# Three hand-written orders for the run-up, the steady and the last bodies of a pipelined transformer block

## The chip, the cores and the metric

The kernel runs on one core of one Trainium2 chip. The metric is the device time of one execution in microseconds. Each kernel is one launch; times are compared between runs on the same chip.

## What is computed

The input is x of 16 batches, 512 tokens each, with 128 features (f32). Three residual steps follow each other:

```python
x = x + linear_attention(layernorm(x)) @ W_out.T   # 16 heads of 8; Chebyshev orders 1..5 of clipped q and k;
                                                   # running sums over the tokens, numerator / denominator
x = x + softmax_attention(layernorm(layernorm(x))) # causal, 16 heads of 8; its own norm with ln1_g, ln1_b
n = layernorm(layernorm(x))                        # last norm with ln2_g, ln2_b
top, idx = top_k(n @ gate_W + gate_b, 2); w = softmax(top)
x = x + sum over the two experts of w * (gelu(n @ W1[e] + b1[e]) @ W2[e] + b2[e])   # 8 experts, 512 hidden
```

## The kernel before

**Two halves.** The first half (until about 1070 us of the trace) runs both attentions and the gate for every batch and sends each token's normed row, with its weight and its number, to a list per expert in HBM (`xg`), by indirect DMAs. The second half runs the experts over 39 blocks of 512 rows from these lists, sends their outputs back to pairs per token, and adds the pairs at the end.

**The software pipeline.** `pipelined(body)` (L327 to L330) calls the body of each engine for t = -5 to 15. One body works on six batches at once, one in each stage; a stage whose batch does not exist is None and is left out:
- f = t+5: first norm (POOL `ln_rsqrt("a")`, ACT `apply0`), projections, clip, and the Chebyshev orders of k and q (`third_order`, `even_orders` L1153/L1154 on POOL, `fifth_order` L536).
- h = t+4: `head_sums` of k and q (PE L1320, ten matmuls of 512 columns on 32 partitions, five for each), `sum_k` (DVE L553, L564), products and running sums (`times_v` L550, `sum_kv` L553, POOL `times_q` L1162, `add_products` L1173), `output1` (L1344, L1355), `add_x1`, the second norm ("m", `ln_rsqrt` in its long form on POOL), ACT `apply1` and `apply2` (both L480; `apply2` writes `ha`).
- g = t+3: `turn_ln`, q, k, v of the softmax attention, and q and k split into three bf16 parts (DVE `third_part` L593, POOL `less_first_part` L1183). SP writes the parts to `spread` in HBM and from there the 'stack' of rows that the scores are products of (L388 to L393); its second half waits until all 48 scores of the body are done.
- m = t+2: the row maxima of the scores, needed ahead of the exponentials. 44 steps: PE `maximum` (L1393, L1395) and DVE's reduction (`nm`, L599). `max_rest` (DVE L602 to L604) and `max_parts` (ACT) turn each half of the maxima into two bf16 rows `nms`, and `put_maxima` (ACT L977) writes them by DMA into the stack. Half 0 belongs to heads 0 to 7, half 1 to heads 8 to 15.
- b = t+1: 48 `scores` (PE L1433, L1435), 48 `exps` (ACT L986), 12 `values` (PE L1452), `evacuate` (ACT L990), four times `turn_back` and `normalise` (DVE L610, L612), `take_y` (ACT L994, the last piece of a batch; its starts mark the bodies here). `scores` 0 waits for half 0 of the stack and of the maxima, `scores` 24 for half 1.
- t: `output2` (PE L1477), `x2` (DVE L621), third norm ("b", POOL L447 to L473), `apply3` (ACT L480, into `rows`), `turn_x2`, gate, `gate_top` and `gate_weights` (DVE L628 to L656), `ranks`, `slots` (DVE L658 to L671, slot numbers `sloti`), ACT `copy_rows` (L1007), and eight indirect DMAs (POOL `dispatch`, L1197), four for each of the two chosen experts, each with 128 rows.

**What sets the order.** Nothing schedules at run time but semaphores: each engine issues its instructions in program order. PE, ACT and DVE walk 129 slots per body. The tables MAX_PE, SCORES_PE, VALUES_PE, MAX_DVE, EXPS_ACT and LEAVE_ACT (L310 to L319) say in which slot each repeated step stands, `at(n, stage)` says it for the single steps, and POOL's and SP's bodies are written out. The order is the same for every t. For example `put_maxima(m, p, 0)` stands at slot 83 of ACT, where 48 of 48 exponentials are already issued.

**The gate's weights.** `gate_weights` computes 1/(1+e) and e/(1+e) in the columns of `gt`, copies both into `rows` (L655), compares the indices with the expert numbers in two instructions (L651), and advances the tokens' numbers in `rows` by 1024 (L656).

## Time and profile before

| what | value |
|---|---|
| device time, median of 3 runs | 1379.57 us (1373.16 to 1382.08) |
| the profiled execution's own time | 1373.93 us |
| span of the profiled execution | 1372.1 us |
| busy, share of the span | PE 83%, DVE 79%, ACT 68%, POOL 61% |
| mean granted TensorE clock | 0.91 |
| run-up bodies (t = -5 to -1) | 0 to 207.4 us |
| steady bodies (t = 0 to 11) | 207.4 to 891.8 us |
| last bodies, three of four (t = 12 to 14), then t = 15 | 891.8 to 1035.3, then to 1070.8 us |
| experts, then the final sums | 1070.8 to 1310, then to 1372.1 us |

PE is TensorE, DVE VectorE, ACT ScalarE, POOL GpSimd, SP SyncE. A body is the stretch from one `take_y` (L994) to the next. PEclk is the granted clock of TensorE as a share of full speed; the two levels are 1.2 and 2.4 GHz, so a stretch at 0.97 spent part of its time at the lower one. A wait in the view of waits names the engine and line that stood idle and what ended it.

### The profile page before, as it was taken

The numbers are of one execution on the slowest core, as the hardware profiler recorded it, in microseconds if no ns is written. First come the engines' busy times: TensorE is split into PE (matmuls) and PEld (weight loads), VectorE is DVE, ScalarE is ACT, GpSimd is POOL, SyncE is SP. The second block draws the span as 40 slices with busy tenths as digits, with TensorE's granted clock in tenths as the row PEclk, the third lists the DMA queues.
The fourth block names the chain that finished last, engine by engine and source line by source line (L and its number), as shares of the span: only waits on it lengthen the run. The fifth ranks groups of instructions, "written<-read, shape, count | busy, mean of one in ns | idle before, by whom it ended". The sixth has DMA issues, their size and how long they took to land.

```text
span 1372.1 us, 27932 instructions
## 1 busy us (share of the span) xinstructions
PE 1141.6 (83%) x8883; PEld 702.2 (51%) x8883; DVE 1086.1 (79%) x2555; ACT 934.1 (68%) x1859; POOL 841.7 (61%) x1105
## 2 busy tenths in 40 slices
PE   3546898998989989889898998988893799999960
PEld 1223354454644546445464454544452588888840
DVE  4557888898988989899898897965715688888845
ACT  2334487696876968769687695675574699999940
POOL 2775566776877767777777686532224166666660
PEclk9677799999999999999999999988985899999985
DMA  9231231423324223142241422413232222222239
GB/s 207 50 88 51 49 88 30 109 72 60 97 51 105 72 58 101 31 115 78 58 103 41 96 77 44 104 62 73 84 127 104 78 79 85 84 86 82 67 139 367
DMA packets 84436, 121.91 MB, mean 89 GB/s; under 512 B 15270, under 2 KB 66522, under 8 KB 80002
## 3 DMA queue, kind: packets, MB, share of 16 engines
q1 hardware_dynamic: 70978, 98.07, 27.5%
q0 software_dynamic: 9088, 17.33, 3.6%
q10 hardware_dynamic: 4224, 4.72, 1.1%
q8 instruction: 71, 1.16, 0.4%
q14 instruction: 75, 0.61, 0.2%
HBM read 63.96 MB, written 57.46 MB: 88 GB/s over the span
## 4 chain that ended last, share of the span: by engine, by line
PE 65%; DMA 12%; DVE 10%; ACT 7%; issue 5%; POOL 1%; ACTq 1%; SPq 0%; POOLq 0%; DVEq 0%
PE back L1452 8%; PE front L1586 8%; PE back L1598 8%; DMA stack<-nms 7%; PE scores L1433 6%; PE front L1320 6%; PE maxima L1393 5%; ACT pr L986 4%; DVE nm L599 3%; PE scores L1435 3%; PE front L1295 3%; PE maxima L1395 3%; PE back L1270 2%; DMA stack<-pairs 2%; PE front L1477 1%
## 5 line engine op out<-in xcount | busy, mean ns | idle before, releaser
L986 ACT ACTIVATE pr<-scores 128x384 f32<-128x384 f32 (+1 forms) x768 | 369.6, 523 | 144.1 <-PE scores L1435 137.3
L599 DVE TENSOR_REDUCE nm<-maxima 128x1 f32<-128x384 f32 (+3 forms) x704 | 420.5, 631 | 44.4 <-PE maxima L1395 38.4
L1433 PE MATMUL scores<-stack 65*128 65x384 bf16 (+2 forms) x768 | 205.6, 285 | 57.3 <-DMA stack<-nms 32.6
L1393 PE MATMUL maxima<-stack 65*128 65x128 bf16 (+2 forms) x768 | 197.7, 282 | 16.2 <-DVE nm L599 14.5
L1197 POOL DMA_INDIRECT xg<-rows,sloti x128 | 137.0, 1070 | 108.0 <-DVE sloti L669 44.0
L1395 PE MATMUL maxima<-stack 128*128 128x128 bf16 x1024 | 182.6, 224 | 6.7 <-DMA stack<-spread 5.1
L1435 PE MATMUL scores<-stack 128*128 128x128 bf16 x1024 | 181.3, 225 | 0.0
L1452 PE MATMUL back<-pr,vaug 128*9 128x512 f32 (+3 forms) x2048 | 178.4, 444 | 1.5 <-ACT oT L990 1.0
L1433 PEld LDWEIGHTS scores<-stack 65*128 65x128 bf16 x768 | 75.6, 98 | 179.3 <-ACT pr L986 106.8
L1259 POOL DMA_INDIRECT pairs<-xs x104 | 111.0, 1068 | 78.7 <-DVE xs L832 51.9
L1393 PEld LDWEIGHTS maxima<-stack 65*128 65x128 bf16 x768 | 74.7, 98 | 121.9 <-DVE nm L599 87.4
L1586 PE MATMUL front<-h_first,w_now 128*128 128x512 f32 x312 | 126.2, 405 | 2.7 <-DVE h_second L812 2.5
L1127 ACT ACTIVATE xs<-front,b1p 128x512 f32<-128x512 f32 x156 | 107.5, 689 | 18.8 <-PE front L1586 16.6
L1162 POOL TENSOR_TENSOR kv<-F,kv 128x512 f32<-128x512 f32 x80 | 100.6, 1283 | 27.6 <-DVE kv L553 27.6
L1395 PEld LDWEIGHTS maxima<-stack 128*128 128x128 bf16 x1024 | 94.5, 100 | 29.9 <-issue 22.0
L1598 PE MATMUL back<-hid_first,w_now 128*128 128x512 f32 x312 | 96.3, 390 | 0.0
L1435 PEld LDWEIGHTS scores<-stack 128*128 128x128 bf16 x1024 | 92.4, 100 | 5.8 <-issue 4.6
L553 DVE TENSOR_TENSOR_SCAN kv<-one,front 128x512 f32<-128x512 f32 x80 | 93.7, 1204 | 0.0
L1320 PE MATMUL front<-F,cst 128*32 128x512 f32 x320 | 81.9, 804 | 3.9 <-DVE F L536 3.5
L1173 POOL TENSOR_TENSOR kv<-kv 128x512 f32<-128x512 f32 x64 | 80.4, 1267 | 2.4
L1153 POOL TENSOR_SCALAR F<-F 128x512 f32<-128x512 f32 x32 | 48.2, 1507 | 53.6 <-DVE F L532 53.3
L825 DVE TENSOR_TENSOR hid_second<-xs,hid_first 128x512 fp32r<-128x512 f32 x99 | 68.0, 687 | 15.7 <-ACT hid_first L1108 14.9
(219 smaller groups left out, 2459.5 us busy)
## 6 DMA issues: line engine op xcount, KB each, us to landing
stack<-spread SPq DMA_DIRECT2D x32, 400.0 KB
spread<-qs SPq DMA_DIRECT2D x96, 128.0 KB
spread<-ks SPq DMA_DIRECT2D x96, 128.0 KB
stack<-spread SPq DMA_DIRECT2D x32, 384.0 KB
xs<-xg SPq DMA_DIRECT2D x39, 272.0 KB, 2.9
stack<-pairs SPq DMA_DIRECT2D x8, 1024.0 KB, 13.5
stack<-in_consts SPq DMA_DIRECT2D x4, 1280.0 KB
xg<-xs SPq DMA_DIRECT2D x17, 272.0 KB
```

Of the source, the lines that this page charges most:

```text
L599: v.tensor_reduce(nm[:, h:h + heads, t], ring(n)[:, 0:heads * (t + 1) * P].rearrange("p (h n) -> p h n", h=heads), AX.X, ALU.max, negate=T ...
L986: a.activation(pr[:, n % PR, 0:width], ringE[n % 2][:, 0:width], ACT.Exp).then_inc(W.exp_ready, 1)
L1197: g_.indirect_dma_start(xg[:, :], bass.IndirectOffsetOnAxis(sloti[:, i, q:q + 1], 0), rows[:, i, q, :], None).then_inc(W.dispatched, 16)
L1259: g_.indirect_dma_start(pairs[:, :], bass.IndirectOffsetOnAxis(xt[i % XT][:, at:at + 1].bitcast(U32), 0), yo[i % 3][:, q * D:(q + 1) * D], ...
L1320: last = k.matmul(dst[32 * j:32 * j + 32, :], cst[:, C_SUM + 32 * var:C_SUM + 32 * var + 32], z[p], start=(p < 4), stop=(p > 0), skip_grou ...
L1393: k.matmul(ring(n)[:, at:at + t * P], qst[p][0:OPEN_ROWS, h, own], kst[p][0:OPEN_ROWS, h, 0:t * P], start=(j == 0), stop=True, skip_group_ ...
L1395: last = k.matmul(ring(n)[:, at + t * P:at + (t + 1) * P], qst[p][:, h, own], kst[p][:, h, own], start=(j == 0 and t == 0), stop=True, ski ...
L1433: k.matmul(dst[:, at + P:at + T - t * P], kst[p][0:OPEN_ROWS, h, own], qst[p][0:OPEN_ROWS, h, (t + 1) * P:T], start=(t == tiles[0]), stop= ...
L1435: last = k.matmul(dst[:, at:at + P], kst[p][:, h, own], qst[p][:, h, own], start=False, stop=True, skip_group_check=True)
L1452: last = k.matmul(V[32 * i:32 * i + DH + 1, t * P:T], vaug[:, b % VR, t, 4 * (s_ // 3) + i, :], pr[:, (4 * s_ + i) % PR, at:at + T - t * P ...
L1586: last = k.matmul((X, Y)[n % 2][:, :], w_now[:, i % 2, wi, c * P:(c + 1) * P], h2p[hi][:, i % 2, :], start=(j == 0), stop=(j == len(TERMS3 ...
L1598: last = k.matmul((Z, V)[i % 2][:, :], w_now[:, i % 2, 2 + wi, c * P:(c + 1) * P], (hidh, hidl)[hi][i % 2 * HC + c], start=(c == 0 and j = ...
```

## The change

- `pipelined` hands each body a number w: 0 for t below 0, 1 for t = 0 to 11, 2 for t = 12 to 15. Every table and every single place becomes a triple, one order for each w.
- GpSimd's body is also placed by slots (26 of them), three orders.
- The places of the split expert weights move (SPLIT_DVE, SPLIT_ACT; only in the body t = 15).
- `gate_weights` writes the reciprocal and the product straight into `rows`, compares with one instruction of 128x64, and leaves the numbers to a new `next_ids` on GpSimd; `dispatch` waits for the weights and the numbers apart.
- `turn_ln` (PE) also waits for `x2` of the batch t.

```diff
-        gt = sb("gt", [P, 4, QT])
+        gt = sb("gt", [P, 2, QT])
...
-        SLOTS = 129
+        SLOTS, POOL_SLOTS = 129, 26
...
-        MAX_DVE = (1, 3, 5, 9, 11, 14, 15, 18, 23, 25, 27, 28, 29, 31, 32, 34, 35, 36, 38, 39, 40, 41, 44, 45, 49, 50, 53, 54, 56, 57,
...
+        MAX_DVE = ((8, 9, 10, 12, 15, 16, 18, 19, 20, 22, 23, 24, 26, 27, 28, 29, 30, 32, 33, 34, 35, 36, 37, 38, 41, 43, 45,
...
...
-        SPLIT_DVE, SPLIT_ACT = (8, 21, 52, 55), (0, 2, 32, 58, 60, 66, 72, 75)
+        SPLIT_DVE, SPLIT_ACT = (20, 36, 45, 52), (17, 24, 58, 64, 76, 80, 84, 87)
...
         def pipelined(body):
 
             for t in range(-5, B):
-                body(*(t + i if 0 <= t + i < B else None for i in range(6)), (t + 1) % 2)
+                body(*(t + i if 0 <= t + i < B else None for i in range(6)), (t + 1) % 2, (t >= 0) + (t >= 12))
...
             def gate_weights(b):
                 dve.wait_ge(W.g_exp, b + 1)
                 v.tensor_scalar(gd[:, :], gt[:, 1, :], 1.0, None, ALU.add).then_inc(W.g_step, 1)
-                dve.wait_ge(W.g_step, b * 4 + 2)
-                v.reciprocal(gt[:, 2, :], gd[:, :]).then_inc(W.g_step, 1)
-                dve.wait_ge(W.g_step, b * 4 + 3)
-                v.tensor_tensor(gt[:, 3, :], gt[:, 1, :], gt[:, 2, :], ALU.mult).then_inc(W.g_step, 1)
+                dve.wait_ge(W.g_step, b * 3 + 2)
+                v.reciprocal(rows[:, 0, :, R_W], gd[:, :]).then_inc(W.g_step, 1)
                 dve.wait_ge(W.topi_ready, b * QT + QT)
-                dve.wait_ge(W.g_step, b * 4 + 4)
-                for i in range(2):
-                    v.tensor_tensor(oh[:, i, :, :], cst[:, C_IO:C_IO + E].unsqueeze(1).to_broadcast((P, QT, E)),
-                                    topi[:, :, i:i + 1].to_broadcast((P, QT, E)), ALU.is_equal).then_inc(W.oh_ready, 1)
-                dve.wait_ge(W.oh_ready, b * 2 + 2)
+                v.tensor_tensor(oh[:, :, :, :], cst[:, C_IO:C_IO + E].unsqueeze(1).unsqueeze(1).to_broadcast((P, 2, QT, E)),
+                                topi[:, :, 0:2].rearrange("p t i -> p i t").unsqueeze(3).to_broadcast((P, 2, QT, E)),
+                                ALU.is_equal).then_inc(W.oh_ready, 1)
+                dve.wait_ge(W.g_step, b * 3 + 3)
+                v.tensor_tensor(rows[:, 1, :, R_W], gt[:, 1, :], rows[:, 0, :, R_W], ALU.mult).then_inc(W.meta_ready, 1)
+                dve.wait_ge(W.oh_ready, b + 1)
                 v.tensor_tensor(chosen[:, :, :], oh[:, 0, :, :], oh[:, 1, :, :], ALU.add).then_inc(W.mask_ready, 1)
-                v.tensor_copy(rows[:, :, :, R_W], gt[:, 2:4, :]).then_inc(W.meta_ready, 1)
-                v.tensor_scalar(rowsi[:, :, :, R_ID], rowsi[:, :, :, R_ID], float(2 * T), None, ALU.add).then_inc(W.meta_ready, 1)
 
...
-                    at = lambda place, stage: n == place and stage is not None
+                    at = lambda places, stage: n == places[w] and stage is not None
...
+                    if at((68, 2, 3), t):
+                        x2(t)
...
+                    if at((1, 4, 81), h):
+                        sum_k(h)
...
+                    if at((40, 45, 47), m):
+                        max_rest(m, 0)
...
+                    if at((51, 80, 19), f):
                         fifth_order(f, kx, W.k_sq, W.k_t35)
...
+                    if at((5, 10, 16), t):
                         apply3(t)
...
+                    if at((28, 49, 36), t):
                         copy_rows(t)
...
+                    if at((77, 75, 70), m):
                         put_maxima(m, p, 0)
...
+            def next_ids(t):
+                if t == 0:
+                    pool.wait_ge(W.meta_ready, 2)
+                g_.tensor_scalar(rowsi[:, :, :, R_ID], rowsi[:, :, :, R_ID], float(2 * T), None, ALU.add).then_inc(W.ids_ready, 1)
+
             sent = [0]
 
             def dispatch(t, i, tiles):
                 wait_apart(pool, W.slot_ready, t + 1)
                 wait_apart(pool, W.h_copied, t + 1)
-                wait_apart(pool, W.meta_ready, t * 2 + 4)
+                wait_apart(pool, W.meta_ready, t + 3)
+                wait_apart(pool, W.ids_ready, t + 1)
...
-            def body(t, b, m, g, h, f, p):
-                if t is not None:
-                    add_residual(t)
-                    ln_rsqrt("b", t)
-                if h is not None:
-                    times_q(h, (0,))
-                if f is not None:
-                    ln_rsqrt("a", f)
-                if h is not None:
-                    times_q(h, (1,))
-                    times_q(h, (2,))
-                    times_q(h, (3,))
-                    times_q(h, (4,))
-                    add_products(h, (0, 1))
-                if g is not None:
-                    less_first_part(g, 0)
-                    less_first_part(g, 1)
-                if h is not None:
-                    add_products(h, (2, 3))
-                if t is not None:
-                    dispatch(t, 0, (0,))
-                    dispatch(t, 0, (1,))
-                    dispatch(t, 0, (2,))
-                if f is not None:
-                    even_orders(f, kx, W.k_t35, W.k_t24)
-                if t is not None:
-                    dispatch(t, 0, (3,))
-                    dispatch(t, 1, (0,))
-                    dispatch(t, 1, (1,))
-                if f is not None:
-                    even_orders(f, qx, W.q_t35, W.q_t24)
-                if h is not None:
-                    ln_rsqrt("m", h)
-                if t is not None:
-                    dispatch(t, 1, (2,))
-                    dispatch(t, 1, (3,))
-                if h is not None:
-                    keep_residual(h)
-                if t is not None:
-                    wait_apart(pool, W.dispatched, t * (16 * 2 * QT) + 16 * 2 * QT)
-                    pool.sem_inc(W.rows_free, 1)
+            def body(t, b, m, g, h, f, p, w):
+                for n in range(POOL_SLOTS):
+                    at = lambda places, stage: n == places[w] and stage is not None
+                    if at((21, 0, 4), t):
+                        ln_rsqrt("b", t)
+                    if at((1, 1, 2), t):
+                        next_ids(t)
+                    if at((2, 2, 3), t):
+                        add_residual(t)
+                    if at((3, 3, 23), f):
+                        ln_rsqrt("a", f)
+                    if at((4, 4, 10), h):
+                        times_q(h, (0,))
+                    if at((6, 5, 22), h):
+                        times_q(h, (1,))
+                    if at((9, 6, 14), h):
+                        times_q(h, (2,))
+                    if at((11, 7, 7), h):
+                        times_q(h, (3,))
+                    if at((16, 8, 8), h):
+                        times_q(h, (4,))
+                    if at((15, 9, 24), h):
+                        add_products(h, (0, 1))
+                    if at((12, 10, 6), g):
+                        less_first_part(g, 0)
+                    if at((18, 11, 15), h):
+                        add_products(h, (2, 3))
+                    if at((14, 12, 9), g):
+                        less_first_part(g, 1)
+                    if at((5, 13, 5), t):
+                        dispatch(t, 0, (0,))
+                    if at((8, 14, 11), t):
+                        dispatch(t, 0, (1,))
+                    if at((7, 15, 12), t):
+                        dispatch(t, 0, (2,))
+                    if at((25, 16, 13), t):
+                        dispatch(t, 0, (3,))
+                    if at((0, 17, 16), t):
+                        dispatch(t, 1, (0,))
+                    if at((10, 18, 17), t):
+                        dispatch(t, 1, (1,))
+                    if at((20, 19, 1), f):
+                        even_orders(f, kx, W.k_t35, W.k_t24)
+                    if at((17, 20, 19), t):
+                        dispatch(t, 1, (2,))
+                    if at((13, 21, 20), t):
+                        dispatch(t, 1, (3,))
+                    if at((22, 22, 18), f):
+                        even_orders(f, qx, W.q_t35, W.q_t24)
+                    if at((23, 23, 21), h):
+                        ln_rsqrt("m", h)
+                    if at((24, 24, 0), h):
+                        keep_residual(h)
+                    if at((19, 25, 25), t):
+                        wait_apart(pool, W.dispatched, t * (16 * 2 * QT) + 16 * 2 * QT)
+                        pool.sem_inc(W.rows_free, 1)
...
-            def turn_ln(g, h):
+            def turn_ln(g, h, t):
                 pe.wait_ge(norm["m"]["out"], g * 8 + 8)
+                if t is not None:
+                    pe.wait_ge(W.x2_ready, t + 1)
                 if h is not None:
...
+                    if at((114, 3, 3), t):
                         output2(t, h)
+                    if at((0, 4, 66), h):
                         head_sums(h, kx, X, W.k_t24, W.k_t35, W.ks_mm, W.x1_ready, h)
+                    if at((2, 5, 17), h):
                         head_sums(h, qx, Y, W.q_t24, W.q_t35, W.qs_mm, *((W.x2_ready, t + 1) if t is not None else (W.outT_ready, h)))
+                    if at((33, 40, 5), g):
+                        turn_ln(g, h, t)
...
```

The orders themselves, as the two programs issue them. First ACT at the end of a steady body. The pr rows are exponentials (`exps`), the DMA rows are `put_maxima`, hs and ha are `apply1` and `apply2`, hn is `take_y`. Before:

```order
L986 ACTIVATE pr<-scores 128x512 x2
L990 ACTIVATE oT<-back 128x512
L986 ACTIVATE pr<-scores 128x384 x8
L977 DMA stack<-nms 1x32x128 x2
L990 ACTIVATE oT<-back 128x512
L480 ACTIVATE hs<-xs,morem,rstdm 128x128 x4
L972 ACTIVATE nms<-back 32x128
L994 ACTIVATE hn<-back 128x512
L977 DMA stack<-nms 1x32x128 x2
L480 ACTIVATE ha<-xs,morem 128x128 x4
```

After:

```order
L1003 ACTIVATE pr<-scores 128x512 x2
L1007 ACTIVATE oT<-back 128x512
L1003 ACTIVATE pr<-scores 128x512
L1003 ACTIVATE pr<-scores 128x384
L994 DMA stack<-nms 1x32x128 x2
L1003 ACTIVATE pr<-scores 128x384 x7
L1007 ACTIVATE oT<-back 128x512
L500 ACTIVATE hs<-xs,morem,rstdm 128x128 x4
L989 ACTIVATE nms<-back 32x128
L1011 ACTIVATE hn<-back 128x512
L994 DMA stack<-nms 1x32x128 x2
```

The first `put_maxima` moved from behind the last exponentials to a place ahead of the last seven; the rest of the body's end is as it was.

Second, PE in the run-up, in the body t = -2, the first that has maxima. The maxima rows are `maximum`, which read the stack, the front rows from L1320 (after: L1358) are `head_sums`. Before:

```order
L1344 MATMUL front<-rdT,cst 128x128 x4
L1355 MATMUL front<-wo_sb,outT 128x128 x4
L1395 MATMUL maxima<-stack 128x128 x4
L1393 MATMUL maxima<-stack 128x128
L1395 MATMUL maxima<-stack 128x128
L1393 MATMUL maxima<-stack 128x128
L1395 MATMUL maxima<-stack 128x128
L1320 MATMUL front<-F,cst 32x512 x5
L1393 MATMUL maxima<-stack 128x128
```

After:

```order
L1382 MATMUL front<-rdT,cst 128x128 x4
L1393 MATMUL front<-wo_sb,outT 128x128 x4
L1358 MATMUL front<-F,cst 32x512 x10
L1435 MATMUL maxima<-stack 128x128 x4
L1433 MATMUL maxima<-stack 128x128
L1435 MATMUL maxima<-stack 128x128
L1433 MATMUL maxima<-stack 128x128
```

All ten matmuls of `head_sums` now stand ahead of the first maximum; before, two maxima steps stood ahead of the first five.

Third, DVE at the gate of a steady body. The nm rows are reductions of the maxima; L643 to L656 (after: L663 to L673) is `gate_weights`. Before:

```order
L599 TENSOR_REDUCE nm<-maxima 128x1
L599 TENSOR_REDUCE nm<-maxima 128x4
L599 TENSOR_REDUCE nm<-maxima 128x2
L643 TENSOR_SCALAR gd<-gt 128x4
L645 RECIPROCAL gt<-gd 128x4
L647 TENSOR_TENSOR gt<-gt 128x4
L651 TENSOR_TENSOR oh<-cst,topi 128x32 x2
L654 TENSOR_TENSOR chosen<-oh 128x32
L655 COPY rows<-gt 128x8
L656 TENSOR_SCALAR rows<-rows 128x8
L599 TENSOR_REDUCE nm<-maxima 128x2
```

After:

```order
L619 TENSOR_REDUCE nm<-maxima 128x2 x2
L663 TENSOR_SCALAR gd<-gt 128x4
L665 RECIPROCAL rows<-gd 128x4
L667 TENSOR_TENSOR oh<-cst,topi 128x64
L671 TENSOR_TENSOR rows<-gt,rows 128x4
L673 TENSOR_TENSOR chosen<-oh 128x32
L619 TENSOR_REDUCE nm<-maxima 128x1 x2
```

Three instructions are gone from DVE (one of two comparisons, the copy and the addition), and the weights are written where the dispatch reads them.

## Rows read from the trace of the kernel before

**Rows 1.** Windows by stage; columns: window, length, busy us and count per engine, PEclk, DMA share.
```profile
0.00:207.40 207.40, 131.87 (x777) 67.05 (x777) 141.02 (x286) 90.65 (x184) 122.55 (x178) 0.79 0.39 89
207.40:891.80 684.40, 625.53 (x5670) 349.51 (x5667) 613.05 (x1535) 510.16 (x1104) 499.48 (x696) 0.97 0.31 75
891.80:1035.30 143.50, 127.88 (x1167) 71.81 (x1164) 73.96 (x225) 92.58 (x198) 39.63 (x58) 0.88 0.30 91
1035.30:1070.80 35.50, 5.65 (x28) 4.60 (x29) 19.41 (x67) 14.24 (x26) 13.97 (x19) 0.51 0.24 84
```

**Rows 2.** Windows of single steady bodies, columns as in rows 1.
```profile
379.50:434.90 55.40, 50.67 (x476) 28.74 (x474) 51.19 (x130) 43.00 (x94) 42.87 (x59) 1.00 0.33 80
...
549.80:608.10 58.30, 53.72 (x476) 29.80 (x474) 51.26 (x130) 43.11 (x94) 42.88 (x59) 0.94 0.31 75
...
720.70:776.50 55.80, 50.82 (x477) 28.80 (x474) 51.33 (x130) 43.16 (x95) 42.26 (x60) 1.00 0.29 74
```

**Rows 3.** Waits of PE, bodies 3 to 12: us in total, times, longest.
```profile
PE scores L1433 <- DMA stack<-nms: 22.8, 10, 2.7
```

**Rows 4.** Chain of waits, 435 to 492 us: start, us, what.
```profile
429.99 7.29 DMA stack<-nms
```

**Rows 5.** Windows around one body's end, columns as in rows 1.
```profile
430.00:433.50 3.50, 3.13 (x34) 1.43 (x30) 3.31 (x9) 1.32 (x3) 2.29 (x10) 1.00 0.91 177
...
439.00:442.00 3.00, 3.00 (x10) 0.35 (x2) 1.09 (x2) 0.51 (x2) 2.34 (x3) 0.52 0.17 52
```

**Rows 6.** Timeline of ACT and POOL, one body's second half: start, us, what.
```profile
403.05 0.48 ACT L986 ACTIVATE pr<-scores 128x384 f32<-128x384 f32 x1
403.42 0.63 ACT L1007 ACTIVATE rows<-rows 128x512 f32<-128x512 f32 x1
...
413.23 1.10 POOL L1197 DMA_INDIRECT xg<-rows,sloti  x1 [0.16 <-issue]
...
419.38 1.51 POOL L1153 TENSOR_SCALAR F<-F 128x512 f32<-128x512 f32 x1 [1.51 <-DVE F L532]
...
437.38 1.65 ACT L480 ACTIVATE ha<-xs,morem 128x128 f32<-128x128 f32 x4 [1.87 <-POOL morem L473]
...
439.43 0.96 POOL L1197 DMA_INDIRECT xg<-rows,sloti  x1 [0.30 <-issue]
```

**Rows 7.** Groups of DVE by line, bodies 3 to 12: busy, mean ns, idle before.
```profile
L599 DVE TENSOR_REDUCE nm<-maxima 128x1 f32<-128x512 f32 (+3 forms) x440 | 262.6, 630 | 10.8 <-PE maxima L1395 6.9 <-DVE xs L584 0.5
...
L553 DVE TENSOR_TENSOR_SCAN ksum<-one,front 128x512 f32<-128x512 f32 x10 | 12.2, 1221 | 16.3 <-PE front L1320 16.3
...
L621 DVE TENSOR_TENSOR x2t<-front,xs 128x512 f32<-128x512 f32 x10 | 6.9, 692 | 18.4 <-PE front L1477 18.4
...
L665 DVE TENSOR_TENSOR oh<-oh,slot 128x64 f32<-128x64 f32 x10 | 3.1, 306 | 0.0
L651 DVE TENSOR_TENSOR oh<-cst,topi 128x32 f32<-128x32 f32 x20 | 2.9, 188 | 1.0
...
L656 DVE TENSOR_SCALAR rows<-rows 128x8 int32<-128x8 int32 x10 | 1.7, 169 | 0.0
L655 DVE COPY rows<-gt 128x8 f32<-128x8 f32 x10 | 1.7, 169 | 0.0
```

**Rows 8.** Groups of POOL by line, same stretch and columns.
```profile
L447 POOL TENSOR_SCALAR lnva<-mva 128x4 f32<-128x4 f32 x9 | 5.1, 569 | 0.8
...
L447 POOL TENSOR_SCALAR lnvb<-mvb 128x4 f32<-128x4 f32 x10 | 2.3, 232 | 30.9 <-DVE mvb L437 30.9
```

**Rows 9.** Waits of PE in the run-up, 0 to 207.4 us.
```profile
PE maxima L1395 <- DMA stack<-spread: 5.1, 1, 5.1
...
PE front L1320 <- DVE F L536: 3.5, 1, 3.5
```

**Rows 10.** Chain of waits, 0 to 208 us.
```profile
60.44 6.56 PE front L1320 x20
```

**Rows 11.** Waits of PE, last three bodies, 891.8 to 1035.3 us.
```profile
PE scores L1433 <- DMA stack<-nms: 5.5, 3, 2.1
```

More of the change, by code:

```diff
@@ L738, in body @@
[L738 to L748 removed]
+                    if at((39, 43, 53), g):
+                        third_part(g, 2, kf, ks)
@@ new lines, in body @@
+                    if at((42, 44, 80), f):
+                        clip(f, kx, W.hk_ev, W.k_clip)
+                    if at((40, 45, 47), m):
+                        max_rest(m, 0)
+                    if at((48, 47, 76), f):
+                        clip(f, qx, W.hq_ev, W.q_clip)
+                    if at((47, 51, 60), g):
+                        third_part(g, 1, qf, qs)
+                    if at((50, 53, 71), f):
+                        third_order(f, kx, W.k_sq, W.k_t35)
+                    if at((44, 54, 49), b):
+                        normalise(b, 0)
@@ L1014, in first_weights, with body @@
                 a.activation(w2p[0][:, e * HC:(e + 1) * HC, :], w2_sb[:, e * HC:(e + 1) * HC, :], ACT.Copy).then_inc(W.wh_ready, 1)
-            def body(t, b, m, g, h, f, p):
+            def body(t, b, m, g, h, f, p, w):
                 for n in range(SLOTS):
-                    at = lambda place, stage: n == place and stage is not None
+                    at = lambda places, stage: n == places[w] and stage is not None
                     if b is None and t is not None and n in SPLIT_ACT:
@@ new lines, in body @@
+            def body(t, b, m, g, h, f, p, w):
+                for n in range(POOL_SLOTS):
+                    at = lambda places, stage: n == places[w] and stage is not None
+                    if at((21, 0, 4), t):
[51 more added lines that the diff above has]
+                        pool.sem_inc(W.rows_free, 1)
@@ L1501, in ranks, with body @@
                 last.then_inc(W.rank_mm, 1)
-            def body(t, b, m, g, h, f, p):
+            def body(t, b, m, g, h, f, p, w):
                 for n in range(SLOTS):
-                    at = lambda place, stage: n == place and stage is not None
-                    if m is not None and n in MAX_PE:
-                        maximum(m, MAX_PE.index(n), 1 - p)
-                    if b is not None and n in SCORES_PE:
-                        scores(b, SCORES_PE.index(n), p)
-                    if b is not None and n in VALUES_PE:
-                        values(b, VALUES_PE.index(n))
-                    if at(3, t):
+                    at = lambda places, stage: n == places[w] and stage is not None
+                    if m is not None and n in MAX_PE[w]:
+                        maximum(m, MAX_PE[w].index(n), 1 - p)
+                    if b is not None and n in SCORES_PE[w]:
+                        scores(b, SCORES_PE[w].index(n), p)
+                    if b is not None and n in VALUES_PE[w]:
+                        values(b, VALUES_PE[w].index(n))
+                    if at((114, 3, 3), t):
```

242 lines of the change are left out of this document (108 added, 134 removed), and 20 rows, old and new, of tables (EXPS_ACT, MAX_DVE, MAX_PE, SCORES_PE).

## The prediction

> **What bounds the kernel now.** I read the windows by stage first, then the waits of PE (TensorE), then the chain of waits, and last the groups by line. In the steady bodies PE is busy 625.5 of 684.4 us, DVE (VectorE) 613.1 [rows 1]. PE is the engine with the least room, and two things stand beside its work. One is a wait in every body: `scores` 0 waits for the DMA of the row maxima, 22.8 us in ten bodies, 2.3 each [rows 3]. The other is its clock: the bodies at clock 1.00 take 55.4 and 55.8 us (first and last of three), one at 0.94 takes 58.3 with DVE's work the same 51.2 to 51.3 [rows 2]. The lower clock comes right behind the wait: at the end of one body PE is at 1.00 (430 to 433.5), and in 439 to 442, behind its wait, at 0.52, so nearly all at 1.2 GHz, with PE busy all the time [rows 5]. So the steady loop loses 2.3 us to the wait, and 57.0 - 55.6 = 1.4 us per body, 17 us in twelve, to the clock (684.4/12 = 57.0; 55.6 is the middle of the two rows).
>
> Why is the DMA late? It takes 7.3 us from issue to landing [rows 4], and it lies in a stretch where the DMA engines are busy 0.91 of the time [rows 5]: SP's loads of the next stack start when the last scores are done, at the same moment. It is issued late because `put_maxima` of half 0 stands behind all 48 exponentials in ACT's order, although the maxima of that half are done far earlier.
>
> **Steady bodies, PE.** The change moves this issue ahead of the last seven exponentials. Seven of them take at least 7 x 0.48 us (one of this shape) [rows 6], and they are paced by PE, so the DMA starts 3.4 us earlier or more, I take 5, out of the crowd; I expect the wait of 2.3 us gone. With it should go the clock's fall. PE's floor is then 55.6 - 2.3 = 53.3 us per body: -3.7, or -44.7 in twelve. That is the upper end of the gain.
>
> **Steady bodies, DVE.** PE won't reach it, since DVE is next: it is busy 51.2 of 57.0, idle 5.8. The edits to the gate take from it the copy (0.169), the addition (0.169), and of two comparisons (2 x 0.188) 0.376 - 0.306 = 0.07, with L665 as the row for an instruction of 128x64: 0.4 us together, at most 0.17 + 0.17 + 0.19 = 0.53, at least 0.34 [rows 7]. Busy is then 50.8. Of the 5.8 us idle, x2's wait for `output2` is 1.8, the first running sum's wait for `head_sums` 1.6, the waits of the maxima's reductions 1.1 [rows 7]; 1.3 is spread. In the new order scores 0, two maxima, `output2` and both `head_sums` open the body, so the two waits at its start shrink (I take 0.4 left of 3.4), but only two maxima stand ahead of the sums; the third and fourth maxima of PE are in slots 12 and 20, and DVE, which gets to them early, will wait for them: about 1.4, and 0.7 more at `max_rest`. With the rest as it is (1.1 + 0.5) this makes 4.1. The body is then 50.8 + 4.1 = 54.9, or -2.1, which is -25.6 in twelve. The ends: nothing if all idle time comes back elsewhere, -44.7 if DVE hides behind PE.
>
> **GpSimd.** `next_ids` is new on POOL: 8 numbers per partition. The nearest rows are POOL's small instructions, 0.23 and 0.57 us [rows 8]; I take 0.4, with 17 us of idle per body (499.5 busy of 684.4 for twelve is 41.6 of 57.0 each) as the cover [rows 1]. If the cover went, it would be 5 us in twelve.
> The row for `lnva` (0.57) against the same operation on `lnvb` (0.23) shows that such an instruction is stretched by what runs beside it [rows 8]. The Trainium skill, "SBUF — State Buffer", section "Who interferes with whom", says why it can: a DVE instruction with two SBUF inputs and a GpSimd instruction that reads SBUF hold one shared port pair by an exclusive lock, and the later of them blocks. By that rule part of the 0.4 us saved on DVE returns as blocking, 0.2 per body, and the sum would be 2.4 us less gain; by the rows alone it is as above.
>
> **Run-up (207.4 us at a clock of 0.79 [rows 1]).** Two waits of PE are aimed at. In the body t = -2 the first maxima wait 5.1 us for the first load of the stack [rows 9]. Now all ten `head_sums` matmuls stand ahead; 20 of them took 6.6 us [rows 10], so 3.3 for each of k and q with the later ones done at once: they fill 4 to 5 of the 5.1. I take -4.5. In an earlier body `head_sums` waits 3.5 us for `fifth_order` [rows 9], which for k now stands behind `third_order` at slot 51 and not at 80; I take -2.5. Sums ahead of maxima on DVE and the rest: -1. Together -8, ends 0 and -15, since the new orders differ in every slot.
>
> **Last bodies (143.5 us, clock 0.88 [rows 1]).** The same DMA costs 5.5 us in three bodies [rows 11], and the clock 127.9 x (1 - 0.88) = 15.3. The wait goes; the clock comes back by half, 7.6, since ACT's exponentials pace these bodies too and small gaps stay. `turn_ln` moves to slot 5 in t = 12, where it waits for x2 and `apply2`: +2. That is -11, ends -3 and -20. The body t = 15 (35.5 us, PE busy 5.7 [rows 1]) is a chain of norm, gate, ranks and eight dispatches; the gate loses 0.4 us of that chain and `next_ids` leaves it: 0 to -1, taken as 0. The experts and final sums are untouched.
>
> **The sum.** -25.6 - 8 - 11 = -44.6 on the profiled execution's own 1373.9 (span 1372.1 and 1.8 around it) is 1329.3. The median of the runs stands 5.7 above that execution, so I put the forecast at 1333, between 1329.3 and the 1335.0 that the median gives.
> By the Trainium skill, "TensorE: Matmul & The Clock Gate", section "HAM oscillation — how this bites in real kernels", the loss is half of the throttled time. In 684.4 us at 0.97, half speed held for 2 x 0.03 x 684.4 = 41 us, so the loss is 20.5 where the bodies' lengths give 17; the sum would be 3 us lower if all of it came back.
>
> **Rivals.**
> (a) PE reaches its floor: DVE's idle time hides and steady bodies take 53.3. For it speaks that PE leads DVE in every view now; against, that DVE would have to be idle for 53.3 - 50.8 = 2.5 us only, less than half of today's 5.8. -44.7 - 8 - 11: 1310 to 1315; with the outer ends of the other two terms, 1298.
> (b) The order gives back what the DMA gave: DVE's new wait for PE's slots 12 and 20, or a maxima DMA that lands no earlier, keeps steady bodies at 57.0, and run-up and last bodies bring half. -9.5: 1370. For it speaks that DVE's idle time is only 5.8 and the new order has new waits. If the wait for stack<-nms still stands in PE's waits, this is the cause.
> (c) Slower: the tail on GpSimd. `copy_rows`, which the dispatches wait for, ran 23.9 us into its body (403.4 - 379.5) [rows 6, 2] with 22 exponentials ahead of it; now 30 stand ahead, which at the same pace is +33.6. Behind it on POOL, in order, stand eight dispatches, both `even_orders` and the norm "m", and then ACT's `apply2` and the exponential 0 of the next body. From the first dispatch to `apply2` was 24.15 us (413.23 to 437.38), less a wait of 1.5; two dispatches stood behind it and were done 3.0 us later (439.43 + 0.96); with `apply2` 1.65 and an exponential 0.5 that is 24.15 - 1.5 + 3.0 + 2.15 = 27.8 [rows 6]. 33.6 + 27.8 = 61.4, or 6.5 us into the next body of 54.9. `output2` and both `head_sums` fill PE until some +6 (1 us and 20 matmuls, 6.6 at half clock, stand in front [rows 10]). So it just fits. If the dispatches, now in one row, cost 0.3 more each, or `copy_rows` slips by 2, PE stands still at scores 2 of every body and its clock falls with each: +3 for the wait and +1.4 for the clock, less the old 2.3: about +2.1 per body or +25, less 8 and 3 elsewhere: 1394. It decides from a tail of 30 us.
> (d) The orders for the run-up and the last bodies bring nothing, those for the steady bodies do: 1373.9 - 25.6 = 1348, by the median 1354.
>
> **How the numbers follow.** Chances: the forecast with its own range of 1320 to 1350, 0.56; (a) 0.09; (b) 0.14; (c) 0.10; (d) 0.11. A measurement of this kernel can tell about 1%, 13.8 us: faster is below 1365.8, slower above 1393.4. Forecast, (a), (d) and a little of (b) are faster, 0.77; the rest of (b) and a part of (c) the same, 0.14; the rest slower, 0.09. The range of 8 in 10 reaches from 1300, most of (a), to 1370, the near half of (b).
>
> **What would show it.** In the profile after: no wait scores <- DMA stack<-nms above 0.3 us per body; granted clock 0.99 or 1.00 in the steady windows; bodies of 54 to 56 us; DVE busy 50.8 in each; reductions (nm) with more idle time before them than 1.1 and `x2` and `ksum` with less; no wait of PE for the stack above 1 us in the run-up; last three bodies some 132 us. A wait of scores <- ACT pr near the start of each body, behind apply2, would show (c). I am wrong if steady bodies stay above 56.5, or if the clock stays below 0.97 with the DMA wait gone.

## The result, and the profile after

The changed kernel took 1344.03 us (median of 4 runs, 1335.16 to 1344.48) beside 1379.02 for the kernel before; the ratio is 0.974, 95% interval 0.9695 to 0.9785. The forecast was 1333 with a range of 1300 to 1370, faster with 0.77. The profiled execution has a span of 1342.3 us, 29.8 less than before.

The windows by stage of the changed kernel (columns as in rows 1):

```profile
0.00:206.50 206.50, 136.72 (x769) 70.07 (x770) 144.42 (x286) 90.52 (x183) 125.30 (x176) 0.77 0.38 89
206.50:871.80 665.30, 619.84 (x5670) 352.98 (x5671) 606.28 (x1500) 514.40 (x1104) 511.15 (x710) 0.97 0.31 77
871.80:1006.30 134.50, 122.77 (x1172) 72.00 (x1170) 73.72 (x215) 92.13 (x197) 40.07 (x63) 0.92 0.33 101
1006.30:1040.00 33.70, 4.73 (x28) 3.76 (x28) 18.88 (x64) 14.24 (x26) 13.54 (x18) 0.57 0.19 65
```

Against rows 1 the run-up gives 0.9 us, the steady bodies 19.1, the last three 9.0 and the body t = 15 1.8; the experts and the final sums take 1.0 more. The granted clock of the steady stage is still 0.97. Three of its bodies, against rows 2:

```profile
315.40:369.60 54.20, 50.34 (x473) 29.07 (x473) 50.51 (x126) 43.28 (x94) 43.68 (x61) 1.00 0.33 80
...
593.50:649.20 55.70, 51.87 (x473) 29.19 (x473) 50.50 (x126) 43.38 (x94) 43.29 (x61) 0.97 0.32 78
649.20:706.10 56.90, 53.15 (x473) 30.28 (x473) 50.60 (x126) 43.45 (x94) 43.36 (x61) 0.94 0.30 75
```

A body at full clock takes 1.2 to 1.6 us less than before, but eight of the twelve still have a part at the lower clock. The waits of PE, bodies 3 to 12, and ACT's wait on GpSimd in the same stretch (us in total, times, longest):

```profile
PE front L1517 <- ACT hn L1011: 14.9, 10, 1.6
PE scores L1473 <- ACT pr L1003: 11.1, 31, 0.5
```

```profile
ACT hs L500 <- POOL morem L491: 18.1, 9, 2.2
```

The wait for the DMA of the maxima [rows 3] is gone. Its place has a new one: `output2` (L1517) waits 1.5 us per body for `take_y` (hn). The timeline of one body's end shows why `take_y` is late (start, us, what, idle before and its releaser):

```profile
478.93 0.33 PE L1473 MATMUL scores<-stack 65*128 65x384 bf16 x1
...
479.07 1.65 ACT L500 ACTIVATE hs<-xs,morem,rstdm 128x128 f32<-128x128 f32 x4 [2.18 <-POOL morem L491]
...
480.62 0.25 ACT L989 ACTIVATE nms<-back 32x128 bf16<-32x128 f32 x1
480.78 0.57 ACT L1011 ACTIVATE hn<-back 128x512 f32<-128x512 f32 x1
...
481.40 1.16 PE L1517 MATMUL front<-wp_sb,hn 128*128 128x128 f32 x8 [1.64 <-ACT hn L1011]
```

ACT stands 2.18 us before `apply1` (hs) until GpSimd's norm m arrives; behind it in ACT's order stand `max_parts` 1 and `take_y`. On GpSimd all eight dispatches and both `even_orders` are now ahead of that norm; before, six of the eight were. This wait is the new order's own. In the kernel before it was 0.5 us per body:

```profile
ACT hs L480 <- POOL morem L471: 4.7, 9, 0.6
```

VectorE's groups, against rows 7 (busy, mean ns, idle before), and the new instruction on GpSimd:

```profile
L619 DVE TENSOR_REDUCE nm<-maxima 128x1 f32<-128x512 f32 (+3 forms) x440 | 262.9, 631 | 21.9 <-PE maxima L1435 18.8 <-issue 0.4
L573 DVE TENSOR_TENSOR_SCAN ksum<-one,front 128x512 f32<-128x512 f32 x10 | 12.0, 1200 | 1.9 <-PE front L1358 1.9
...
L641 DVE TENSOR_TENSOR x2t<-front,xs 128x512 f32<-128x512 f32 x10 | 6.9, 691 | 5.8 <-PE front L1517 5.8
...
L624 DVE TENSOR_TENSOR nms<-back,nms 32x128 bf16<-32x128 f32 x11 | 3.1, 279 | 12.3 <-ACT nms L989 12.3
...
L667 DVE TENSOR_TENSOR oh<-cst,topi 128x64 f32<-128x64 f32 x10 | 1.9, 195 | 0.0
```

```profile
L1205 POOL TENSOR_SCALAR rows<-rows 128x8 int32<-128x8 int32 x10 | 3.6, 358 | 0.8
```

VectorE's two waits at the body's start (x2 and the first running sum) fell from 3.5 us to 0.8 together, the maxima's rose from 1.1 to 2.2, and `max_rest` 1 waits 1.2 behind the same `apply1`.

### The profile page after: what moved, and what is told of

Read it like the earlier page. It is cut to its first block, busy times and chain, and to the rows that moved or that the text cites. A ratio compares the mean times of both kernels' runs of the same rounds, so it can differ in the third digit from the quotient of the medians.

```text
span 1342.3 us, 28013 instructions
## 1 busy us (share of the span) xinstructions
PE 1135.3 (85%) x8883; PEld 708.5 (53%) x8883; DVE 1081.7 (81%) x2507; ACT 937.8 (70%) x1859; POOL 856.1 (64%) x1121
## 4 chain that ended last, share of the span: by engine, by line
PE 59%; DVE 11%; POOL 10%; issue 7%; ACT 7%; DMA 4%; POOLq 0%; SPq 0%; ACTq 0%; DVEq 0%
PE front L1626 8%; PE back L1638 8%; PE back L1492 7%; PE scores L1473 5%; PE front L1358 5%; DVE nm L619 5%; PE maxima L1433 4%; POOL xg L1220 3%; ACT pr L1003 3%; PE scores L1475 3%; POOL F L1170 2%; PE maxima L1435 2%; DMA stack<-pairs 2%; PE back L1308 2%; DMA xg<-rows,sloti 1%
## 5 line engine op out<-in xcount | busy, mean ns | idle before, releaser
L1220 POOL DMA_INDIRECT xg<-rows,sloti x128 | 137.3, 1073 | 118.2 <-issue 53.8
L1492 PE MATMUL back<-pr,vaug 128*9 128x512 f32 (+3 forms) x2048 | 184.1, 461 | 0.0
L1179 POOL TENSOR_TENSOR kv<-F,kv 128x512 f32<-128x512 f32 x80 | 106.9, 1357 | 23.0 <-DVE kv L573 23.0
L1125 ACT ACTIVATE hid_first<-xs 128x512 fp32r<-128x512 f32 x117 | 74.1, 633 | 3.7
L1297 POOL DMA_INDIRECT pairs<-pr,xs x52 | 55.1, 1059 | 26.9 <-DVE pr L849 12.3
```

What stands on the lines that cost most here:

```text
L1220: g_.indirect_dma_start(xg[:, :], bass.IndirectOffsetOnAxis(sloti[:, i, q:q + 1], 0), rows[:, i, q, :], None).then_inc(W.dispatched, 16)
L1297: g_.indirect_dma_start(pairs[:, :], bass.IndirectOffsetOnAxis(xt[i % XT][:, at:at + 1].bitcast(U32), 0), yo[i % 3][:, q * D:(q + 1) * D], ...
L1492: last = k.matmul(V[32 * i:32 * i + DH + 1, t * P:T], vaug[:, b % VR, t, 4 * (s_ // 3) + i, :], pr[:, (4 * s_ + i) % PR, at:at + T - t * P ...
```

## The experiments

Two theories stand against each other. **Tail theory:** from GpSimd's first dispatch to `take_y` a steady body takes 22.7 us; the starts lie at +31.5 and +54.2 us in the clean bodies and 22.7 apart in the slower ones too; GpSimd's tail (what it does from that dispatch to norm m) sets the new wait, and the wait the clock. **VectorE theory:** the forecast's own, 50.8 us of work and 4.1 of idle time set the body.

The first four kernels ran on a chip on which the kernel before takes 1417.8 us, the other eight on two chips where it takes 1379.2 and 1383.8, like that of the result. All ratios are to the kernel before on the same chip.

**apply1 behind take_y**

```diff
-                    if at((84, 84, 13), h):
+                    if at((84, 89, 13), h):
                         apply1(h)
```

> Changed kernel with one edit in the steady bodies: ACT issues apply1 behind max_parts 1, take_y and put_maxima 1, not ahead of them. Tail theory (GpSimd's tail of dispatches, even orders and norm m holds apply1, and take_y stands behind it, so output2 is late by 1.5 us in each body): the wait output2 <- take_y (14.9 us in ten bodies) falls below 3; the tail itself still ends in apply2 and the first exponential, so 1.0 to 1.3 us of it comes back as a wait of scores for pr; steady bodies 665.3 -> 655 to 661, time -4 to -10 against 1344. DVE theory (the forecast's: 50.8 us of work and 4.1 us of idle time at the maxima set the body): steady bodies within 2 us of 665.

1371.9 us, ratio 0.9726 (0.9662 to 0.979). The wait for `take_y` is gone and the five bodies at clock 1.00 take 54.8 to 55.2 us, but in the other seven the clock fell, mostly from +40 us on behind waits in mid-body, and the steady stage took 689.3. As the changed kernel had not run on this chip, the times could not be told apart; so the kernel ran again, below.

**Two dispatches behind norm m**

```diff
-                    if at((17, 20, 19), t):
+                    if at((17, 24, 19), t):
                         dispatch(t, 1, (2,))
...
-                    if at((13, 21, 20), t):
+                    if at((13, 24, 20), t):
                         dispatch(t, 1, (3,))
```

> Changed kernel with one edit in the steady bodies: the last two dispatches stand behind norm m on GpSimd, as in the kernel before. Tail theory: norm m, apply1 and take_y come 2.4 us earlier, the wait output2 <- take_y goes (under 3 us in ten bodies), PE's clock stays at 1.00 in most bodies: 665.3 -> 640 to 652, time -13 to -25 against 1344; against it works that the next body's norm b then waits for the dispatches' landing (0.4 us per body in the kernel before). DVE theory: within 2 us of 665.

1399.2 us, ratio 0.9886 (0.9846 to 0.9926): a miss in time, with a steady stage of 709.4 us where the tail theory had 640 to 652. The waits of PE and ACT, ten bodies:

```profile
PE scores L1473 <- ACT pr L1003: 27.4, 32, 3.2
...
PE front L1517 <- ACT hn L1011: 0.4, 2, 0.2
```

```profile
ACT rows L500 <- POOL moreb L491: 26.3, 10, 2.7
```

The wait for `take_y` went as the tail theory says. But norm b is now late behind the dispatches of the last body, `apply3` (rows) stands at slot 10 of ACT and holds it for 2.6 us, and the exponentials behind it hold PE. The old order had `apply3` four slots later.

**copy_rows earlier and later**

```diff
-                    if at((28, 49, 36), t):
+                    if at((28, 41, 36), t):
                         copy_rows(t)
```

The second kernel has (28, 55, 36) there.

> Changed kernel with copy_rows at slot 41 in the steady bodies (49), some 4 us earlier. If copy_rows sets the first dispatch (the slower rival of the prediction), the dispatches start up to 1 us earlier and the body follows: 665 -> 650 to 655. If GpSimd's own queue (its two subtractions end at +31.1 us, the dispatch starts at +31.5) and the slot numbers set it, the first dispatch moves by under 0.4 us: 661 to 665. DVE theory: no change.

> Changed kernel with copy_rows at slot 55 in the steady bodies (49), some 2 to 3 us later. Tail theory: the first dispatch moves by as much, and with the fixed 22.7 us behind it the body does: +1.5 to +3 us per body and the clock falls in every one, steady bodies 665 -> 690 to 705, time 1370 to 1385. DVE theory: the tail has slack, steady bodies under 670.

Earlier: 1401.6 us, ratio 0.9903 (0.9867 to 0.9939), steady stage 713.4. Later: 1385.3, ratio 0.9783 (0.9736 to 0.983), steady stage 700.4. The first dispatch of one body each, from the timelines of GpSimd; the bodies of the changed and the later kernel are at clock 1.00, and the earlier kernel has none that is. The changed kernel (its body starts at 315.4, `copy_rows` at 345.37), the earlier one (259.1, 285.68) and the later one (318.4, 351.67):

```profile
345.36 1.16 POOL L1200 TENSOR_TENSOR kf<-kf,ks 128x512 f32<-128x512 f32 x1
346.94 1.10 POOL L1220 DMA_INDIRECT xg<-rows,sloti  x1 [0.43 <-issue]
```

```profile
289.11 1.16 POOL L1200 TENSOR_TENSOR kf<-kf,ks 128x512 f32<-128x512 f32 x1
290.44 1.10 POOL L1220 DMA_INDIRECT xg<-rows,sloti  x1 [0.17 <-issue]
```

```profile
353.22 1.44 POOL L1220 DMA_INDIRECT xg<-rows,sloti  x1 [3.68 <-ACT rows L1024]
```

Moved up by 3.4 us (from +30.0 to +26.6), `copy_rows` lets the first dispatch start only 0.2 earlier, as GpSimd is busy with its subtraction until then: `copy_rows` was not what the tail waited for, and the slower rival of the prediction named the wrong head of the tail. Moved down by 3.3, it becomes just that: GpSimd waits 3.68 for it, the dispatch starts at +34.8, and the body is 56.6 at clock 1.00 where the changed kernel's is 54.2. That the tail made this body longer is not shown, though: PE hardly waits for `take_y` in this kernel (3.0 us in ten bodies). In this body it stands 1.5 us in mid-body for a reduction of the maxima.

That the earlier one was slower than the later one neither theory expected. All its steady bodies lie at clocks of 0.91 to 0.94, mostly with the lower one from +37 to +43 us on, behind two or three waits of 0.4 to 2.1 us there. Such waits belong to this chip as much as to the edits: in ten bodies of the kernel with apply1 moved, PE waits 16.0 us for VectorE's reductions here and 3.7 when the same kernel runs on another chip. The profile also puts waits of ACT and VectorE in these four kernels down to "remote" (a releaser that it cannot name, 22.9 us of ACT in ten bodies of the earlier kernel), and none in the other eight. What it is stays open, and with it how much of the four times is the edits'.

**put_maxima back, and put_maxima alone**

```diff
-                    if at((77, 75, 70), m):
+                    if at((77, 83, 70), m):
                         put_maxima(m, p, 0)
```

In the kernel before, alone:

```diff
-                    if at(83, m):
+                    if at(75, m):
                         put_maxima(m, p, 0)
```

> The changed kernel itself, as the control of this call: the first call's kernels ran on a chip where the kernel before takes 1417.8 us, not 1379. If the chip shifts everything alike, the ratio to the kernel before is 0.974 again (0.970 to 0.979). If the steady bodies of the changed kernel owe their length to TensorE's clock falling behind small waits, and that differs between chips, the ratio moves by over 0.005 and the share of bodies at clock 1.00 with it.

> Changed kernel with put_maxima 0 of the steady bodies back behind all 48 exponentials (slot 83, was 75). If the early issue of this DMA is what the steady gain rests on: the wait scores <- DMA stack<-nms is back at 2 to 4 us per body, the clock falls in every body, steady bodies 25 to 35 us longer than the changed kernel's, ratio to the kernel before 0.99 to 1.00. If the rest of the new order brings the gain: under 8 us of it is lost, ratio under 0.98.

> Kernel before with one edit: put_maxima 0 between exponentials 40 and 41 (slot 75, was 83), in all bodies. If the early DMA is the change's gain: the DMA wait (2.3 us per body) is gone, most bodies run at clock 1.00, steady bodies 684 -> 655 to 670, last three 143.5 -> 134 to 139, ratio 0.970 to 0.985. If the new orders are needed for it, the wait passes to x2, the sums or take_y: steady bodies above 676, ratio 0.985 to 1.0.

The control, which is the changed kernel again: 1343.4 us, ratio 0.975 (0.9671 to 0.9828). Back: 1382.7, ratio 1.0024 (0.9987 to 1.0061), all of the gain lost. Alone: 1337.6, ratio 0.9693 (0.9625 to 0.976), all of the gain kept. With the edit undone, the waits of PE:

```profile
PE scores L1473 <- DMA stack<-nms: 32.0, 9, 4.2
```

3.6 us each and a steady stage of 705.2 us at 0.93: the new order needs this DMA earlier than the old one did, as its scores 0 are PE's first instruction of a body. With the edit alone, the steady stage and the last three bodies:

```profile
208.75:860.39 651.64, 610.50 (x5670) 343.30 (x5668) 618.88 (x1535) 511.68 (x1104) 500.74 (x696) 1.00 0.32 79
860.39:999.74 139.35, 122.16 (x1168) 68.72 (x1165) 74.04 (x225) 92.81 (x197) 39.55 (x58) 0.95 0.31 93
```

All twelve steady bodies are at clock 1.00, 54.3 us on average, 32.8 less than before in the stage, better than the 655 to 670 expected. Five of the twelve take 53.5 to 53.8 us, at the floor of the prediction, with VectorE busy 51.0 to 51.2 in them. Its waits of PE, in ten bodies and the 9 us behind them (in the ten alone the first row is 17.0 us, the longest 1.9):

```profile
PE scores L1433 <- ACT pr L986: 19.9, 34, 2.6
PE back L1270 <- DVE yt L612: 6.0, 10, 0.6
...
PE front L1477 <- ACT hn L994: 2.1, 10, 0.2
```

In the old order `take_y` comes in time (0.2 us per body), though the DMA wait is gone there as well. The place of one instruction is the whole steady gain, and the rest of the change to the steady bodies takes 14 us of it back (665.3), in the controls 19 to 22 (673.4, 670.8). How that divides between the other places and the new gate is in the next two parts.

**The gate as before**

The edit takes back `gate_weights`, the size of `gt`, and the waits of the weights, and drops `next_ids`:

```diff
-                    if at((1, 1, 2), t):
-                        next_ids(t)
...
-                wait_apart(pool, W.meta_ready, t + 3)
-                wait_apart(pool, W.ids_ready, t + 1)
+                wait_apart(pool, W.meta_ready, t * 2 + 4)
```

> Changed kernel with the old gate: gate_weights with its copy, its two comparisons and the addition of the numbers on VectorE, no next_ids on GpSimd; orders as changed. VectorE gets some 0.5 us more per body, GpSimd 0.3 less. GpSimd's tail or PE as the bound: steady bodies within 3 us of the changed kernel's, time within 3. VectorE as the bound (the forecast's term): +0.4 to +0.7 per body, +5 to +8 in all.

1333.9 us (1328.9 to 1343.1), ratio 0.9651 (0.9583 to 0.972), 9.5 us below the control; both theories missed it. The profiled execution is the slowest of its four. Its steady bodies are 55.1 us on average (661.6 in the stage, 673.4 in the control), eight of twelve at 1.00. VectorE is busy 52.1 us per body and not 50.6, yet `output2` waits 0.25 us for `take_y`, no longer 1.5. By their means over ten bodies the steps of the tail explain 1.0 of these 1.25 us: the eight dispatches take 1.02 us each and not 1.09, and the step of norm m that `apply1` waits for (`morem`) 0.20 and not 0.62. Why the same instructions take less time is taken up below.

**The old steady order with the new ends**

This kernel has the steady places of the kernel before with `put_maxima` 0 at 75, the changed kernel's for the run-up and the last bodies, and the old gate; the second has the new gate. Two of its triples, against the changed kernel's:

```diff
-                    if at((81, 3, 5), t):
+                    if at((81, 7, 5), t):
                         stats3(t)
...
-                    if at((5, 10, 16), t):
+                    if at((5, 14, 16), t):
                         apply3(t)
```

> Kernel before with the one early put_maxima in its steady order, the changed kernel's orders for the run-up and the last bodies, and the old gate. If the new run-up and last orders are worth what the windows of the changed kernel's runs show (run-up 201 to 206.5 against 208.8, last three 130.6 to 134.5 against 139.4 in the run with put_maxima alone): 8 to 15 us under that run, 1323 to 1330 by a kernel before of 1379, ratio 0.959 to 0.965. If those gains hang on the new steady order (the bodies at the joints), ratio 0.967 or above.

> As x1_old_steady_new_ends, with the new gate and next_ids on GpSimd. If the new gate costs by itself (the changed kernel with the old gate came out 9 us faster): 5 to 10 us slower than x1. If it only cost there because VectorE's earlier steps met the new steady order's tail: within 3 us of x1, steady bodies 0.3 shorter on VectorE.

> The kernel of e1_apply1_behind_take_y again, beside the changed kernel on one chip. If the wait of output2 behind take_y costs the changed kernel its clock: steady bodies 54.8 long at clock 1.00 where its own are 55.4 to 56.1, 6 to 15 us under the changed kernel. If another wait takes its place in mid-body (the maxima's reductions, +37 to +42 us into the body in the first run): within 4 us of it.

> The changed kernel as control of this call: ratio to the kernel before 0.970 to 0.979 where the chip behaves as in the second call; its steady bodies wait 1.5 us for take_y before output2 and lose the clock behind it in two of three bodies.

- With the old gate: 1330.2 us (1325.3 to 1333.5), ratio 0.9625 (0.9573 to 0.9677), as expected if the new ends keep their gain. It beats the kernel before and the changed one: 12.8 us under the control, and all its runs lie below all of the control's. That it beats put_maxima alone is not shown, as the two ran on different chips and their intervals overlap.
- With the new gate: 1337.5 (1334.5 to 1343.7), ratio 0.9679 (0.9631 to 0.9727), 7.3 us above it.
- apply1 behind take_y: 1345.2, ratio 0.9731 (0.9682 to 0.978).
- Control: 1343.0 (1339.2 to 1345.5), ratio 0.9717 (0.9667 to 0.9768).

The stages of the best one:

```profile
0.00:198.76 198.76, 128.34 (x769) 66.64 (x770) 144.69 (x286) 90.80 (x183) 127.07 (x176) 0.82 0.41 93
198.76:857.31 658.55, 615.00 (x5673) 345.61 (x5674) 621.50 (x1535) 512.73 (x1104) 507.96 (x699) 0.99 0.32 78
857.31:992.43 135.12, 124.23 (x1170) 71.08 (x1166) 75.16 (x225) 92.35 (x197) 40.89 (x59) 0.91 0.33 101
```

So in the steady stage the new order costs 7.7 us with the new gate (670.8 in the control against 663.1), and 10.0 with the old one (661.6 against 651.6 with put_maxima alone, which has the old ends too).

Moving `apply1` alone moves the wait: it leaves `output2` and stands at +5.4 us, at scores 2, for the first exponential behind `apply2`. The waits of PE, ten bodies, and a clean body and one behind it:

```profile
PE scores L1473 <- ACT pr L1003: 23.2, 41, 1.4
```

```profile
425.04:478.39 53.35, 50.69 (x475) 29.11 (x474) 51.05 (x127) 43.49 (x94) 42.46 (x58) 1.00 0.34 82
478.39:534.67 56.28, 52.88 (x475) 29.81 (x474) 51.32 (x127) 43.85 (x94) 43.55 (x61) 0.94 0.32 78
```

One body reaches 53.35, the PE floor of the prediction. Ten of the others have a wait of 1.4, and this is the only one of twelve at 1.00.

The new gate beside the old one in the old steady order, VectorE's groups in bodies 3 to 11. With the old gate, then with the new:

```profile
L558 DVE SCALAR_TENSOR_TENSOR front<-F,va 128x512 f32<-128x512 f32 x45 | 36.1, 838 | 0.0
...
L645 DVE TENSOR_TENSOR gt<-top 128x4 f32<-128x4 f32 x9 | 6.7, 742 | 0.9
```

```profile
L558 DVE SCALAR_TENSOR_TENSOR front<-F,va 128x512 f32<-128x512 f32 x45 | 40.4, 932 | 0.0
...
L645 DVE TENSOR_TENSOR gt<-top 128x4 f32<-128x4 f32 x9 | 9.2, 1025 | 0.9
...
L655 DVE TENSOR_TENSOR oh<-cst,topi 128x64 f32<-128x64 f32 x9 | 2.7, 301 | 0.0
```

Three instructions are gone and VectorE is busier (626.3 us in the stage against 621.5): the same products take 0.93 us and not 0.84, and a difference of 4 numbers 1.03 and not 0.74. The Trainium skill, "SBUF — State Buffer", section "Who interferes with whom", has the rule: a VectorE instruction with two SBUF inputs and a GpSimd one that reads SBUF exclude each other. These two have such inputs, and the stretches agree with it; that the lock is the cause was not tried by itself.

## Why the prediction was right or wrong

**The bound and the cause: right.** The late DMA and the clock behind it were the loss. Undone, the gain is gone; alone, it gives 32.8 us in the stage, between the forecast's 25.6 and the floor's 44.7.

**The size of the steady term: 25.6 forecast, 19.1 measured (11.0 and 13.6 in the controls).** The failed step is "With it should go the clock's fall". The body at full clock is 54.2, even under the 54.9 that I reckoned, but the clock still falls in eight of twelve bodies: 665.3 - 12 x 54.2 = 15 us. The new order brings its own wait, 1.5 us at `output2`; with put_maxima alone it is 0.2. I should have asked for each PE instruction at the new start of the body what it waits for.

This wait is only a part of the cause. In the three profiles of the changed kernel the clock fell in 27 of the 30 bodies that have it, but also in four of the six that don't (t = 0 and t = 4), where PE stands 0.6 us at most. In these it falls at +8 to +9 us, behind a stretch in which PE is paced by the exponentials and busy 1.26 of 2 us. The body t = 4 of the first control (its start is 427.9):

```profile
433.91:435.91 2.00, 1.26 (x9) 0.52 (x10) 1.87 (x7) 1.95 (x5) 1.36 (x5) 1.00 0.00 0
435.91:437.91 2.00, 2.00 (x16) 0.61 (x18) 2.00 (x3) 1.84 (x6) 1.84 (x3) 0.61 0.00 0
```

Whether this stretch costs the clock was not tried.

**VectorE as the next engine: the sum was near, the conclusion not.** Idle time of 4.1 was forecast, and 55.4 - 50.5 = 4.9 measured per body. The waits that the sum names came out at 4.2 (nm 2.2, x2 0.6, ksum 0.2, `max_rest` 1.2) where it had 3.6, and 0.7 is spread. For the spread part the sum took 0.5 where its own rows had 1.3, without a reason. But the kernel with put_maxima alone runs faster with VectorE busy 51.6 us per body (618.9/12) and not 50.5, and the old gate's extra work did no harm. VectorE's load by itself does not set the body. Rival (a) was refused because VectorE would have to be idle for 2.5 us only; in the five shortest bodies with put_maxima alone it is idle for 2.5 to 2.7.

**The slower rival: the mechanism was right, its place and price not.** The tail on GpSimd is the new wait. It meets PE at `apply1` and `take_y`, one step before the first exponential, and its head is GpSimd's own queue, not `copy_rows`: at +30.0 it came earlier than the forecast +33.6. I priced it at 4.4 us per body, 3 of wait and 1.4 of clock; it measured 1.5 and at most 15/12 = 1.25, 2.7 together, still under the 3.7 of the old wait and its clock, so it took gain back and did not turn the sign. The rival's own sum was wrong too: from the 4.4 it took only the old wait of 2.3 and not the old 1.4 of clock, which the 57.0 hold as well. With it the price is 0.7 per body, some +8 us, and not +25.

**The gate: sized right, its sign in doubt.** 0.4 us was forecast; 0.34 and 0.376 - 0.195 = 0.18 make 0.52 less, VectorE's busy time fell from 51.2 to 50.5. `next_ids` took 0.358, forecast 0.4. Yet in two pairs, each on one chip, the kernel with the new gate is the slower one, by 9.5 and 7.3 us. In the second pair the profiled run-ups differ by 8 us though no gate runs there, so what of it is the gate's stays open; the steady stage shows 4.5 (663.1 against 658.6), and 11.8 in the first pair.

**Run-up: 8 forecast, 0.9 measured, 4.9 and 5.5 in the controls.** The two waits are gone as forecast, and the third batch's `head_sums` start at 95.6 us, not 102.3. The chains of waits, before and after:

```profile
102.33 3.55 PE front L1320 x10
```

```profile
95.62 5.73 PE front L1358 x20
```

But sums ahead of the maxima cost PE this wait in 100 to 165 us, the body t = -2 above all (the longest is 6.4 us), where it was 10.8 in the kernel before:

```profile
PE maxima L1433 <- DVE nm L619: 19.2, 19, 6.4
```

"Sums ahead of maxima on DVE and the rest: -1" had the wrong sign. The rest is the clock: of twelve profiled run-ups in this order nine took 198.8 to 203.1 us at a clock of 0.80 to 0.82, and three 206.3 to 206.9 at 0.77. Two in the old order took 207.4 at 0.79 and 208.8 at 0.76. Why a run-up falls into one group or the other is open.

**Last bodies: 11 forecast, 9.0 measured, 12.9 and 10.2 in the controls.** Right; `turn_ln` waited 1.9 us, 2 forecast. Put_maxima alone, which moved the DMA in these bodies too, gave 4.2.

**The whole.** The forecast of 1333 was 11 us too low. On the profiled execution the run-up is short by 7.1 us, the steady bodies by 6.5 and the last ones by 2.0.

## What to carry to other kernels

Look at the wait that stands at the start of every loop body and ask for the single instruction whose place causes it; try that move alone before a new order for everything. Here it gave all of the steady gain, and the rest of the change gave a part back. A new order brings its own waits: for each instruction that it moves to the start of a body, read what that instruction waits for and what stands ahead of that on the other engine. The same instruction can take different times in different orders: with three instructions less on VectorE, GpSimd's tail was 1.0 us longer here. So count the waits behind a saving and not only the saving.

## What the runs showed of the hardware

- The longest time of PE without a matmul in a steady body, and how many of the twelve bodies are at clock 1.00:

| kernel | longest time | bodies at 1.00 |
|---|---|---|
| put_maxima alone | 1.1 us or less in eleven, 1.9 in one | 12 |
| changed kernel, and its two controls | 1.6 in ten of each | 4, 0, 1 |
| apply1 behind take_y, second run | 1.4 in ten | 1 |
| kernel before | 1.8 to 2.7 in all | 3 |
| put_maxima back | 3.1 to 4.2 in eleven | 0 |

- I had not expected the full clock to be lost as often with a wait of 1.4 to 1.6 us as with one of 2.3. The longest wait alone does not tell it: bodies of the changed kernel with none above 0.6 us lost it in four cases of six, and one body with put_maxima alone kept it behind 1.9.
- The same kernel before took 1379 us on some chips and 1417.8 on another, with the other kernels longer as well, and one and the same kernel had 16.0 us of PE waits for reductions on that chip and 3.7 on another.
